# A macaron stack on one core: pieces of the routing placed elsewhere in the mixing tail, marks by units, an own order for the first beats of the last stage

## The chip, the cores and the metric

The kernel runs on one core of one Trainium2 chip. The metric is the time of one execution on the device in microseconds (us); the number compared is the median of several runs. TensorE is called PE, VectorE DVE, ScalarE ACT, GpSimd POOL and SyncE SP, as in the profile.

## The reference, cut to what matters

The input is 4 x 1024 tokens of 128 features. Six layers follow each other, each with a layer norm in front and a residual sum behind:

```python
x = x + 0.5 * moe(ln(x))        # run 0: shared MLP + the two best of 8 experts (128 -> 512 -> 128)
x = x + mix(ln(x))              # 8 heads: h = tanh(a) * h + b along the sequence, then an FFN with gelu
x = x + 0.5 * moe(ln(x))        # run 1: the same MoE weights again
x = x + 0.5 * ternary_ffn(ln(x))    # L1, first half
x = x + linear_attention(ln(x))     # L1: Z = cumsum(v k^T), y = q Z, 16 heads of 8
x = x + 0.5 * ternary_ffn(ln(x))    # L1, second half
```

The MoE's gate is `topk_p, topk_i = top_k(softmax(xf @ Wr), 2)`, so the logits of a token decide which experts' lists it stands in.

## The kernel before, in words

The residual X stays in SBUF. Its 32 blocks of 128 tokens are worked on as TILES = 8 tiles of four blocks (512 columns). Every engine runs a program of its own; the order in each is written out by hand, and engines wait for each other by semaphores. The queues are in order, so a wait holds up all that stands behind it on its engine.

**A MoE run** begins with the routing. For each tile: `find_stats` (L353, DVE), `find_rstd` (L363, POOL: one addition of EPS and one power of -1/2, over the tile's four columns), `normalize_for_route` (L369, DVE, four instructions), `turn_for_route` (L375, PE transposes, from line L193), `copy_for_route` (L381, ACT), `find_logits` (L385, PE, four products of 8 columns, L389). When all eight tiles have logits, `route` (L660, DVE) picks two experts for each token, `find_places` (L394, PE) counts, and `find_spots` (L678, DVE) gives each (token, expert) pair its spot in the lists. Then the lists are inverted: for each of UNITS = 16 units of four columns of spots, `mark` (L707, DVE) writes four pairs of one-hot matrices in f16, `marks_lo` (128 wide, from the spot's low part) and `marks_hi` (92 wide, from its high part, times the token's number), and `add_marks` (L400, PE, L403) adds up their products in one bank. `keep_rows` (L716, DVE) turns the sum into row numbers, with which POOL gathers the lists by indirect DMA (L586).

The marks are spread over the steps of the shared MLP (a step is one `up` and one `down` of a 128-wide chunk, L424 and L437): `units_at` (L318) places units from step 6 in run 0 and from step 8 in run 1, three units for two steps, and `rows_at` places `keep_rows` ten steps behind the first unit's last neighbour. In run 0, DVE and ACT also split the raw expert weights into high and low parts at the even steps (`split_weights`, L499 on ACT, L768 on DVE). After the shared steps of six tiles come 23 lists of 512 rows, then two more shared tiles.

**The mixing** (`mix_pe`, `mix_act`, `mix_pool`, `mix_dve`) runs over 78 slots: 64 slots (HEADS), one for each head of each tile, and 14 more in which tile 7's remaining work runs out: `z_root` (L1292, POOL), `normalize_z` (L1223, ACT), `u_of` (L1416, DVE), `turn_u`, `up`, `down` (L1111, L1117, PE) with `gelu` (L1238, ACT), `h_of` (L1404, DVE), `y_of` (PE), `add_to_x` (L1425, DVE). In these last slots the routing of run 1 is already interleaved for tiles 0 to 6. The placing before is a staircase, one tile a slot:

```python
STATS_AHEAD, NORM_AHEAD, TURN_AHEAD, LOGITS_AHEAD = (HEADS + k for k in (2, 3, 4, 5))
```

Tile i has its stats and its root in slot 66 + i, its normalization in 67 + i, its transpose in 68 + i and its logits in 69 + i. Tile 7's routing waits for the last `add_to_x`, which ends the mixing (`phase_done`); PE does two `up` steps of run 1 ahead of it.

**L1** is one loop over beats (`l1_pe` L1547, `l1_act` L1695, `l1_pool` L1767, `l1_dve` L1835). Tile i does each piece of work at beat lag + 4 i:

```python
ADD_ROWS, STATS_1, TURN_1, UP_1, DOWN_1, BACK_1, TURN_LA, VK, QS, CHUNK_0 = range(10)
```

ADD_ROWS adds the experts' rows of the MoE (`moe_combine`, L652 on DVE, after POOL has fetched them by indirect DMA, L642); STATS_1 to BACK_1 are the first ternary FFN (its `ff_add` is L1847); TURN_LA takes the tile to the attention; VK and QS are its four projections (L1594, L1596, L1608); from CHUNK_0 on, one chunk of 128 tokens a beat is summed: `products` (L1797, POOL), `sums` (L1617, PE), `read_out` (L1863, L1866, DVE). `root` (L1779 to L1784, POOL) stands in front of each normalization (L1691, ACT). In a beat, POOL issues two fetches (from beat 2 on) ahead of the roots of that beat.

## Time and profile before

| | |
|---|---|
| median of 3 runs | 1185.23 us (1183.57 to 1189.68) |
| the profiled execution: its time, its span | 1186.23 us, 1184.5 us |
| busy: PE, DVE, ACT, POOL | 1066.8, 840.4, 669.8, 683.2 us |
| mean granted clock of PE | 0.954 of full speed |
| marks of run 0, run 1 | about 46 to 86 us, 661 to 690 us |
| mixing | about 270 to 642 us, its tail from 600 us |
| L1 | from about 866 us to the end |

The profiled execution takes 1.73 us more than its span, and 1.0 us more than the median. A busy share is an average over stages; which engine's wait ends last is read stage by stage. A granted clock of 0.50 is 1.2 GHz, 1.00 is 2.4 GHz. DMA-issuing instructions on POOL (L586, L642) appear with the time that POOL spends on them.

### The profile page before, as it was taken

The numbers are of one execution on the slowest core, as the hardware profiler recorded it, in microseconds if no ns is written. First come the engines' busy times: TensorE is split into PE (matmuls) and PEld (weight loads), VectorE is DVE, ScalarE is ACT, GpSimd is POOL, SyncE is SP. The second block draws the span as 40 slices with busy tenths as digits, with TensorE's granted clock in tenths as the row PEclk, the third lists the DMA queues.
The fourth block names the chain that finished last, engine by engine and source line by source line (L and its number), as shares of the span: only waits on it lengthen the run. The fifth ranks groups of instructions, "written<-read, shape, count | busy, mean of one in ns | idle before, by whom it ended". The sixth has DMA issues, their size and how long they took to land.

```text
span 1184.5 us, 16414 instructions
## 1 busy us (share of the span) xinstructions
PE 1066.8 (90%) x4800; PEld 731.3 (62%) x4800; DVE 840.4 (71%) x2362; ACT 669.8 (57%) x1265; POOL 683.2 (58%) x786
## 2 busy tenths in 40 slices
PE   6779999998989999999979979999967678999996
PEld 6336778875657677667745448888734445555553
DVE  6785787767867887787765967777762676767661
ACT  2336767765566676667543338777744445545533
POOL 4006556637998888877662046666465665754330
PEclk9989999999999999999987989999996888989998
DMA  8666667741000000000001036877510000000000
GB/s 270 240 261 210 213 214 246 239 127 29 14 14 13 14 14 12 15 5 1 1 19 54 1 117 213 252 241 241 162 53 19 16 16 25 25 12 10 10 18 18
DMA packets 67976, 108.81 MB, mean 92 GB/s; under 512 B 8336, under 2 KB 46224, under 8 KB 67856
## 3 DMA queue, kind: packets, MB, share of 16 engines
q1 hardware_dynamic: 57904, 87.30, 22.1%
q0 software_dynamic: 9984, 20.47, 6.8%
q8 instruction: 39, 0.64, 0.2%
q14 instruction: 49, 0.40, 0.1%
HBM read 81.00 MB, written 28.57 MB: 93 GB/s over the span
## 4 chain that ended last, share of the span: by engine, by line
PE 58%; POOL 17%; DVE 11%; issue 6%; ACT 5%; DMA 2%; POOLq 0%; SPq 0%; DVEq 0%; ACTq 0%
PE bank L193 7%; PE bank L426 3%; PE bank L427 3%; PE bank L428 3%; PE bank L443 3%; PE bank L445 3%; PE bank L444 3%; POOL wr L642 3%; PE bank L1071 3%; PE bank L1077 3%; PE bank L1596 3%; PE bank L424 2%; PE bank L1111 2%; PE bank L1617 2%; POOL got L642 2%
## 5 line engine op out<-in xcount | busy, mean ns | idle before, releaser
L586 POOL DMA_INDIRECT spare_all<-xs,list_row x184 | 191.7, 1042 | 210.9 <-DVE list_row L724 107.4
L781 DVE TENSOR_TENSOR hid_lo<-hid,hid_hi 128x512 fp32r<-128x512 f32 x184 | 127.0, 692 | 75.0 <-ACT hid L528 73.4
L528 ACT ACTIVATE hid<-bank,b_up_of 128x512 f32<-128x512 f32 x184 | 125.6, 684 | 6.5 <-PE bank L428 1.2
L527 ACT ACTIVATE hid_hi<-bank,b_up_of 128x512 fp32r<-128x512 f32 x138 | 95.3, 690 | 47.7 <-PE bank L428 35.2
L642 POOL DMA_INDIRECT got<-ys,y_slots x80 | 87.3, 1091 | 51.0 <-issue 40.7
L193 PEld LDWEIGHTS bank<-ident,spare_all 128*128 128x128 f32 x504 | 64.8, 150 | 78.0 <-issue 57.6
L193 PE MATMUL bank<-ident,spare_all 128*128 128x128 f32 x504 | 82.1, 289 | 26.1 <-DVE spare_all L372 18.0
L1190 ACT ACTIVATE gate_b<-bank,head_rstd 128x128 f32<-128x128 f32 x256 | 73.0, 370 | 55.7 <-POOL head_rstd L1297 55.2
L528 ACT ACTIVATE hid<-bank,cols_sb 128x512 f32<-128x512 f32 x64 | 43.9, 687 | 88.4 <-PE bank L424 79.4
L426 PE MATMUL bank<-xh,wr 128*128 128x512 f32 x184 | 82.4, 448 | 3.5 <-DVE xl L774 3.5
L1863 DVE TENSOR_TENSOR gate_b<-bank,spare_all 128x512 f32<-128x512 f32 x64 | 43.1, 687 | 50.2 <-PE bank L1617 48.0
L443 PE MATMUL bank<-hid_hi,wr 128*128 128x512 f32 x184 | 76.0, 413 | 0.0
L1297 POOL TENSOR_TENSOR head_rstd<-head_var,neg_half 128x4 f32<-128x4 f32 x64 | 72.4, 1131 | 5.3
L424 PE MATMUL bank<-xT,w_shared 128*128 128x512 f32 x128 | 73.1, 661 | 0.8 <-DVEq L1473 0.8
L427 PE MATMUL bank<-xh,wr 128*128 128x512 f32 x184 | 73.0, 397 | 0.0
L428 PE MATMUL bank<-xl,wr 128*128 128x512 f32 x184 | 72.8, 396 | 0.0
L445 PE MATMUL bank<-hid_lo,wr 128*128 128x512 f32 x184 | 72.6, 394 | 0.0
L444 PE MATMUL bank<-hid_hi,wr 128*128 128x512 f32 x184 | 72.5, 394 | 0.0
L1071 PE MATMUL bank<-spare_all,cw_sb 128*128 128x512 f32 x128 | 66.9, 604 | 3.3 <-DVE spare_all L1398 3.2
L1077 PE MATMUL bank<-wz,spare_all 128*128 128x128 f32 x512 | 68.3, 276 | 1.6 <-ACT gate_b L1190 1.6
L437 PE MATMUL bank<-hid,w_shared 128*128 128x512 f32 x128 | 66.7, 611 | 0.0
L1042 PE MATMUL bank<-xh,hid_hi 128*128 128x512 f32 x136 | 65.6, 483 | 1.1 <-DVE xl L1352 0.9
(291 smaller groups left out, 2749.0 us busy)
## 6 DMA issues: line engine op xcount, KB each, us to landing
wr<-wq SPq DMA_DIRECT2D x92, 512.0 KB, 4.7
ys<-spare_all SPq DMA_DIRECT2D x46, 256.0 KB, 5.3
wq<-wr SPq DMA_DIRECT2D x16, 512.0 KB, 5.7
got<-in_w_mlp SPq DMA_DIRECT2D x8, 512.0 KB, 5.9
xs<-spare_all SPq DMA_DIRECT2D x16, 256.0 KB, 2.3
spare_all<-xs,list_row POOLq DMA_INDIRECT x184, 3.7
out_x<-X SPq DMA_DIRECT2D x8, 256.0 KB, 2.3
ys<-in_x SPq DMA_DIRECT2D x1, 1792.0 KB, 10.5
```

Of the source, the lines that this page charges most:

```text
L193: ins = nc.tensor.transpose(out[:, b * P:(b + 1) * P], src(b), ident[:])
L426: nc.tensor.matmul(out[:], w_up(j, 0, c), xh[:, j % 2], start=True, stop=False)
L427: nc.tensor.matmul(out[:], w_up(j, 1, c), xh[:, j % 2], start=False, stop=False)
L428: nc.tensor.matmul(out[:], w_up(j, 0, c), xl[:, j % 2], start=False, stop=True).then_inc(s["up_done"], 1)
L443: nc.tensor.matmul(out[:], w_dn(j, 0, c), hid_hi[:, q], start=(c == 0), stop=False)
L444: nc.tensor.matmul(out[:], w_dn(j, 1, c), hid_hi[:, q], start=False, stop=False)
L445: nc.tensor.matmul(out[:], w_dn(j, 0, c), hid_lo[:, q], start=False, stop=(c == HC - 1)).then_inc(s["down_done"], 1)
L528: nc.scalar.activation(hid[:, n % HC], bank[up_bank(n)][:], ACT.Gelu_apprx_tanh, bias=bias).then_inc(s["gelu_done"], 1)
L586: g.indirect_dma_start(out=xin[:, j % XIN, b], out_offset=None, in_=xs, in_offset=bass.IndirectOffsetOnAxis(ap=list_row[:, n:n + 1], axis=0))\
L642: nc.gpsimd.indirect_dma_start(out=rows_of(i, ring)[:, k, b], out_offset=None, in_=ys, in_offset=bass.IndirectOffsetOnAxis(ap=y_slots[:, k ...
L781: v.tensor_tensor(hid_lo[:, q], hid[:, n % HC], hid_hi[:, q].bitcast(F32), ALU.subtract).then_inc(s["lo_done"], 1)
L1077: ins = nc.tensor.matmul(blk(bank[3 + q % 2], b), blk(o_sb[:, q % 2], b), wz[:, q % NH], start=True, stop=True)
```

## The change: what it does, and the diff

- **Tail.** The staircase is replaced by tables. Stats of tiles 0 to 5 stand in slots 64 to 66, two a slot; one `find_rstd` over 24 columns serves these six tiles in slot 66; tiles 0 to 2 and 3 to 5 are normalized together in slots 67 and 69; only tiles 0 to 3 are turned in the tail (slots 69 and 72), with logits in slots 70, 71, 75 and 76, now ahead of the turns in a slot. Tiles 4 to 6 are turned, and get their logits, at the head of run 1, ahead of tile 7; the four first `up` steps come behind tile 7's logits.
- **Marks.** `marks_hi` is laid out with the unit's four columns innermost, so that one `tensor_tensor` makes it for a whole unit (368 elements in f16, one operand broadcast); the token's number moves to `marks_lo`. PE reads `marks_hi` with a step of four elements. `find_spots` gets one small copy (`spot_hi16`), the constants one more.
- **L1.** In beats 0 to 8 (`fills`) PE and ACT go in an own order: the attention's turn and projections come ahead of the FFN's work of the next tile, and the sums of chunk 0 stand in beat 8 between Q and QT. POOL issues no fetch in beats 2 to 4; the eight of tile 2 come in beat 5 behind that beat's roots, none in beats 6 and 7, two in beat 8, four each in beats 9 and 10, two from then on. Tile 1's rows are added in beat 5, behind tile 0's stats, in place of beat 4.

```diff
-        def find_rstd(pool, steps, s, i):
-            tile = slice(i * TB, (i + 1) * TB)
-            pool.wait_ge(*s.at("stats_ready", i + 1))
...
+        def find_rstd(pool, steps, s, i, tiles=1):
+            those = slice(i * TB, (i + tiles) * TB)
+            pool.wait_ge(*s.at("stats_ready", i + tiles))
+            steps.link(nc.gpsimd.tensor_scalar(ve_all[:, those], mv_all[:, those, 1], EPS, None, ALU.add))
+            nc.gpsimd.tensor_tensor(rstd_all[:, those], ve_all[:, those], neg_half[:, 0:tiles * TB], ALU.pow).then_inc(s["rstd_ready"], tiles)
...
-                for n in range(2):
-                    step(n)
-                turn_for_route(pe, s, TILES - 1)
+                for i in range(TURNED_AHEAD, TILES):
+                    turn_for_route(pe, s, i)
+                    if i > TURNED_AHEAD:
+                        find_logits(pe, s, i - 1)
                 find_logits(pe, s, TILES - 1)
-                for n in range(2, HC):
+                for n in range(HC):
                     step(n)
                 find_places()
...
-                for m in range(TB):
-                    at = u * TB + m
-                    v.tensor_scalar(marks_lo[:, u % 2, m], column_no16[:], spot_lo[:, at:at + 1], None, ALU.is_equal)
-                    ins = v.tensor_scalar(marks_hi[:, u % 2, m], column_no16[:, 0:COLUMNS], spot_hi[:, at:at + 1],
-                                          token_no[:, at % BLOCKS:at % BLOCKS + 1], ALU.is_equal, ALU.mult)
+                at = u * TB
+                by_block = spot_hi16[:, at:at + TB].unsqueeze(1).broadcast_to([P, COLUMNS, TB])
+                v.tensor_tensor(marks_hi[:, u % 2], column_by_block[:], by_block, ALU.is_equal)
+                for n in range(at, at + TB):
+                    ins = v.tensor_scalar(marks_lo[:, u % 2, n - at], column_no16[:], spot_lo[:, n:n + 1],
+                                          token_no[:, n % BLOCKS:n % BLOCKS + 1], ALU.is_equal, ALU.mult)
...
-        STATS_AHEAD, NORM_AHEAD, TURN_AHEAD, LOGITS_AHEAD = (HEADS + k for k in (2, 3, 4, 5))
+        TURNED_AHEAD, NORMED_AHEAD, ROOTS_AHEAD = 4, TILES - 1, TILES - 2
+        STATS_AHEAD = {HEADS: (0, 1), HEADS + 1: (2, 3), HEADS + 2: (4, 5), HEADS + 6: (6,)}
+        NORMS_AHEAD = {HEADS + 3: (0, 1, 2), HEADS + 5: (3, 4, 5), HEADS + 7: (6,)}
+        TURNS_AHEAD = {HEADS + 5: (0, 1), HEADS + 8: (2, 3)}
+        LOGITS_AHEAD = {HEADS + 6: (0,), HEADS + 7: (1,), HEADS + 11: (2,), HEADS + 12: (3,)}
...
+                if n == HEADS + 2:
+                    find_rstd(pool, steps, after, 0, ROOTS_AHEAD)
+                if n == HEADS + 6:
+                    find_rstd(pool, steps, after, ROOTS_AHEAD)
...
+        def parts_at(beat):
+            if beat < CHUNK_0 - 4:
+                return []
+            if beat == CHUNK_0 - 4:
+                return range(TOP * TB, 2 * TOP * TB)
+            first = {CHUNK_0 - 3: 0, CHUNK_0 - 2: 0, CHUNK_0 - 1: 2, CHUNK_0: 4, CHUNK_0 + 1: 4}
...
+                if fills(beat):
+                    if here(TURN_LA) is not None:
+                        l1_take(pe, s, here(TURN_LA), 1, bank[4])
+                    if here(VK) is not None:
+                        project(here(VK), V)
+                        project(here(VK), K)
+                    if here(BACK_1) is not None:
+                        ff_back(here(BACK_1), 0)
+                    if here(QS) is not None:
+                        project(here(QS), Q)
+                        sums(0)
+                        project(here(QS), QT)
+                    if here(UP_1) is not None:
+                        ff_up(here(UP_1), 0)
+                    if here(DOWN_1) is not None:
+                        ff_down(here(DOWN_1), 0)
+                    if here(TURN_1) not in (None, 0):
+                        ff_turn(here(TURN_1), 0)
+                    continue
-                if g is not None:
+                if g is not None and g > 0:
                     sums(g)
...
                     l1_stats(dve, steps, s, here(BACK_1), 1)
+                    if fills(beat):
+                        moe_combine(dve, steps, moe, 1, FETCHED_WIDE)
...
-                if here(ADD_ROWS) not in (None, 0):
+                if here(ADD_ROWS) not in (None, 0, 1):
```

## Rows read from the trace of the kernel before

**Rows 1.** The page's chain that ended last, shares of the span by engine.

```profile
PE 58%; POOL 17%; DVE 11%; issue 6%; ACT 5%; DMA 2%; POOLq 0%; SPq 0%; DVEq 0%; ACTq 0%
```

**Rows 2.** The same chain in order of time, run 0: start, us, what.

```profile
45.12 1.23 DVE wr L768
...
52.39 1.23 DVE wr L768
```

**Rows 3.** Groups by line, DVE, 28 to 110 us: count, busy us, mean ns, idle before.

```profile
L712 DVE TENSOR_SCALAR marks_hi<-column_no,spot_hi,token_no 128x92 f16<-128x92 f16 x64 | 19.5, 304 | 0.0
L711 DVE TENSOR_SCALAR marks_lo<-column_no,spot_lo 128x128 f16<-128x128 f16 x64 | 16.0, 250 | 0.0
...
L697 DVE TENSOR_TENSOR gate_b<-pick,place 128x512 f32<-128x512 f32 x1 | 0.7, 693 | 0.0
...
L728 DVE TENSOR_TENSOR past<-block_no,ends 128x184 f32<-128x184 f32 x1 | 0.3, 344 | 0.0
```

**Rows 4.** Busy time by window, marks of run 1: length, PE, PEld, DVE, ACT, POOL, PEclk, DMA.

```profile
664.00:689.50 25.50, 23.86 (x120) 11.92 (x119) 23.20 (x117) 9.08 (x14) 0.00 (x0) 1.00 0.00 1
```

**Rows 5.** Timeline of the mixing tail and run 1's first work: start, us, engine, line.

```profile
603.95 0.89 DVE L1367 BATCH_NORM_STATS2 o_stats<-bank 128x6 f32<-128x128 f32 x4 [1.45 <-PE bank L193]
...
607.98 0.23 POOL L1296 TENSOR_SCALAR head_var<-o_mv 128x4 f32<-128x4 f32 x1
...
611.93 0.87 DVE L1409 BATCH_NORM_STATS2 z_stats<-pick 128x6 f32<-128x128 f32 x4 [2.90 <-POOL pick L1306]
612.18 1.04 POOL L367 TENSOR_TENSOR rstd_all<-ve_all,neg_half 128x4 f32<-128x4 f32 x1
...
619.90 0.68 DVE L1419 TENSOR_TENSOR t_sb<-t_sb,rows_sb 128x512 f32<-128x512 f32 x1
...
621.36 1.12 PE L193 MATMUL bank<-ident,t_sb 128*128 128x128 f32 x4 [0.47 <-DVE t_sb L1420]
...
624.86 3.60 PE L1111 MATMUL bank<-acc,f_sb 128*128 128x512 f32 x4
...
638.01 1.90 PE L389 MATMUL bank<-cols_sb,xT 128*128 128x8 f32 x16
...
641.46 0.69 DVE L1425 TENSOR_TENSOR X<-bank,X 128x512 f32<-128x512 f32 x1 [3.06 <-PE bank L1049]
...
648.80 0.42 DVE L667 TENSOR_REDUCE top<-bank 128x32 f32<-128x256 f32 x1 [2.48 <-PE bank L389]
```

**Rows 6.** Groups by form, POOL, whole span: count, busy us, mean ns, idle before.

```profile
L1306 POOL TENSOR_TENSOR pick<-pick,gate_b 128x512 f32<-128x512 f32 x32 | 50.3, 1572 | 19.7 <-ACT gate_b L1190 18.9
...
L1783 POOL TENSOR_TENSOR l_shift<-l_mv,l_rstd 128x4 f32<-128x4 f32 x24 | 4.8, 201 | 1.9
L367 POOL TENSOR_TENSOR rstd_all<-ve_all,neg_half 128x4 f32<-128x4 f32 x16 | 16.6, 1037 | 1.3
```

**Rows 7.** PE: timeline of run 0's routing, then two windows (PEclk is 0.50).

```profile
15.50 1.71 PE L389 MATMUL bank<-cols_sb,xT 128*128 128x8 f32 x8
17.07 1.09 PE L193 MATMUL bank<-ident,spare_all 128*128 128x128 f32 x4
...
642.00:644.00 2.00, 1.74 (x2) 0.84 (x3) 1.41 (x9) 0.00 (x0) 0.19 (x1) 0.50 0.00 0
...
904.00:906.00 2.00, 2.00 (x8) 1.34 (x7) 1.97 (x7) 0.59 (x1) 0.00 (x0) 0.50 0.00 0
```

**Rows 8.** Timeline of L1's first beats.

```profile
883.05 0.69 DVE L1847 SCALAR_TENSOR_TENSOR X<-bank,X 128x512 f32<-128x512 f32 x1 [0.15 <-DVE X L652]
...
884.10 0.94 POOL L642 DMA_INDIRECT wr<-ys,y_slots  x1 [0.30 <-issue]
...
888.86 0.23 POOL L1779 TENSOR_SCALAR l_ve<-l_mv 128x4 f32<-128x4 f32 x1
...
890.91 0.23 POOL L1779 TENSOR_SCALAR l_ve<-l_mv 128x4 f32<-128x4 f32 x1
...
908.56 2.09 POOL L1797 TENSOR_TENSOR wa_sb<-spare_all 128x512 f32<-128x512 f32 x2 [10.71 <-ACT spare_all L1725]
```

More of the change, by code:

```diff
@@ L540, in step @@
                     nc.scalar.activation(half_tanh[:], lead[:], ACT.Tanh, scale=0.5).then_inc(s["tanh_ready"], 1)
-            for i in range(TILES if first else 0):
+            for i in range(0 if first else TURNED_AHEAD, TILES):
                 copy_for_route(act, s, i)
-                if i in (4, 6):
+                if first and i in (4, 6):
                     split_weights(i // 2 - 2)
             for n in range(STEPS + TAIL):
-                if not first and n == 2:
-                    copy_for_route(act, s, TILES - 1)
                 if n == STEPS + HC:
@@ L1264, in mix_act @@
                     gelu(two_before, 1)
-                if tile_ahead(n, TURN_AHEAD) is not None:
-                    copy_for_route(act, after, tile_ahead(n, TURN_AHEAD))
+                for i in TURNS_AHEAD.get(n, ()):
+                    copy_for_route(act, after, i)
         def mix_pool(pool, steps, s, moe, after):
@@ L1464, in mix_dve @@
                     u_of(before_it)
-                if tile_ahead(n, NORM_AHEAD) is not None:
-                    if n == NORM_AHEAD:
-                        dve.wait_ge(s["p_in"], HEADS)
-                    normalize_for_route(dve, after, tile_ahead(n, NORM_AHEAD))
-                if tile_ahead(n, STATS_AHEAD) is not None:
-                    find_stats(dve, steps, after, tile_ahead(n, STATS_AHEAD))
+                if n == max(NORMS_AHEAD):
+                    dve.wait_ge(s["p_in"], HEADS)
+                for i in NORMS_AHEAD.get(n, ()):
+                    normalize_for_route(dve, after, i)
+                for i in STATS_AHEAD.get(n, ()):
+                    find_stats(dve, steps, after, i)
             dve.wait_ge(s["tile_done"], TILES)
@@ L1498, in chunk_at, with fills @@
             return g if 0 <= g < CHUNKS else None
+        def fills(beat):
+            return beat < CHUNK_0
+        def parts_at(beat):
[4 more added lines that the diff above has]
+            first = {CHUNK_0 - 3: 0, CHUNK_0 - 2: 0, CHUNK_0 - 1: 2, CHUNK_0: 4, CHUNK_0 + 1: 4}
+            at = 2 * TOP * TB + sum(n for b, n in first.items() if b < beat) + 2 * max(0, beat - CHUNK_0 - 2)
+            return [n for n in range(at, at + first.get(beat, 2)) if n < TOP * TB * (TILES - 1)]
         kv = [w[:].rearrange("p (h a) e -> p h (a e)", h=2) for w in (wa, wb)]
@@ L1805, in l1_pool @@
                     products(chunk_at(beat + 1))
-                ahead, part_no = divmod(2 * beat + TOP * TB // 2, TOP * TB)
-                if beat > STATS_1 and ahead + 1 < TILES:
-                    for n in (part_no, part_no + 1):
-                        moe_fetch(pool, moe, ahead + 1, n, FETCHED_WIDE)
+                if not fills(beat):
+                    for n in parts_at(beat):
+                        moe_fetch(pool, moe, 1 + n // (TOP * TB), n % (TOP * TB), FETCHED_WIDE)
                 if here(BACK_1) is not None:
```

52 lines of the change are left out of this document (36 added, 16 removed).

## The prediction, made before the change was run

> **What bounds the kernel now.** I read the page's chain first: PE carries over half of it, POOL and DVE the next shares [rows 1]. So the time is a relay, and each of the three edits must be priced in its own stage. The chain in order of time shows run 0's marking: two splits of weights on DVE start 7.27 us apart, and between them lie the sixteen mark instructions of two units [rows 2]. In run 1 the window of the marks shows PE busy 23.86 of 25.50 us and DVE 23.20: PE loses 1.64 us to waits, and no more can be won there [rows 4]. The timeline of the tail shows a relay for tile 7, from its stats at 611.93 to the sum at 641.46 to 642.15, and then 6.65 us until the routing starts at 648.80 [rows 5]. In L1's first beats, the root of tile 0 starts at 888.86 although the FFN's sum ended at 883.74: POOL was still issuing fetches [rows 8].
>
> **Marks.** A unit is now four pairs of instructions. Their mean durations are 0.304 and 0.250 us [rows 3]; on the timeline consecutive ones overlap by about 0.09, so they start 0.21 and 0.16 apart, and four pairs take 1.50 us. After the change four `marks_lo` have two operations: they cost like today's `marks_hi`, 4 x 0.22 = 0.88. The new `tensor_tensor` has 368 elements of f16. No row shows a two-source f16 instruction. By 32-bit elements it lies between the 184 and the 512 columns of [rows 3]: 0.344 + 184 x (0.693 - 0.344) / 328 = 0.54 us, 0.45 without the overlap. By bytes, 368 f16 elements are the 184-column f32 row: 0.34, or 0.25. I take the bytes, because today's `marks_lo`, wider than `marks_hi`, is not longer, so columns of f16 can't cost a full step each. A unit then takes 1.13 us instead of 1.50 (0.37 less; 0.17 by elements).
> The Trainium skill (VectorE: DVE Perf Modes, the rule on which mode an instruction takes) lets `tensor_tensor` handle two elements a cycle if all tensors are 16-bit with step one, and never more. By it the unit is the 1.13 above; no run here shows it yet.
> Run 0: five splits are followed by two units each on the chain (from 45.12 on, period 7.27), 10 x 0.37 = **3.7 us**; by elements 1.7. The units at odd steps hide behind the split on ACT. The splits' loads and stores on SP's queue are asked for two periods ahead, which covers a period shorter by 0.7. Run 1: three units take 3.4 us of DVE for two steps of PE, which take 4.4; so DVE stops being the bound and PE regains nearly all of its 1.64: **1.5 us**, with either price. The copy in `find_spots` (0.2) is hidden: in run 0 by the split that follows, in run 1 by PE's steps. The constant is made before the routing, in DVE's wait for logits. `keep_rows`, POOL's gather and the first list follow the marks in both runs, so both gains pass on.
>
> **Tail, DVE and POOL.** Stats of tiles 0 and 1 (1.25 us each) now stand ahead of the last head's stats. These started at 603.95 and ended 2.7 us before POOL took them at 607.98 [rows 5]; they end 1 us later, so nothing moves. Stats 2 to 5 (5.0 us) end at 611.1, and z's stats still start when POOL's last addition is done, 611.93. Then POOL runs the root over 24 columns ahead of z's root. Its price is the unknown. The power over 4 columns takes 1.04 us, a multiplication over 4 takes 0.20 [rows 6]. If width is free: 1.04. If the extra 0.84 grows with the columns: 0.2 + 6 x 0.84 = 5.2 us. An addition over 512 columns takes only 1.57, so the engine has a cheap loop, but the power's loop is not shown. I take 2.0 us, nearer the row of the same operation, and keep both ends. z's root then starts 0.9 later than before.
> **Tail, u to X.** Before, u's first product waited at 619.90 behind other tiles' normalizations, though its input was ready near 617.9; PE then had turns and logits of tiles 1 to 6 between the pieces of the FFN, which began at 624.86 after the turn at 621.36, at a slow clock (3.60 us for four half-matmuls) [rows 5]. After, u's product follows at 617.4 + 0.9; the turn of u ends 1.6 earlier than before; 1.6 us of logits and turns leave the gap in front of `up`, 1.1 the gap in front of its second half, 1.2 that between the `down`s, and the 1.9 us of L389 at 638.01 no longer stand between `h_of` and `y_of` (1.4 of them were on the path). Less one turn or logits that remains in each of two gaps, the last sum comes 5.6 us earlier.
> **Tail, what is late next.** Behind the sum, PE still has logits 2 and 3, then turns 4 to 6 and logits 4 and 5 before tile 7's turn. At full clock (0.43 and 0.87 a tile) this ends just when tile 7 is normalized, 4.2 us after the sum. But in run 0 the same stretch of turns and logits alone runs at 2.45 us a tile, half speed, from end to end [rows 7]; and before the change the clock was down at 642, after some 4 us of small products [rows 7]. The work left over (four turns at 0.89, four logits at 1.57) then takes 9.8 us from about 1.2 after the sum: the routing starts 11.0 behind the sum instead of 6.65, and the four `up` steps, two of them slow, end about when `route` does. That costs 4.4 to 5.7; I take 5.0. Tail: 5.6 - 5.0 = **0.6 us** gained (free width and free clock: 6.5 to 7; 5.2 us for the root: -2.5).
>
> **L1.** After: POOL is free when tile 0's stats are done, so that root starts near 884.9 instead of 888.86, and the first turn of the attention goes into PE's empty time. Tile 1's rows (2.3 us of DVE) now lie between the two stats, so tile 1's root starts at 888.5 instead of 890.91: 2.4 us earlier [rows 8]. From there PE is busy without a break and at a clock of 0.50 [rows 7], and its work up to tile 1's FFN sum is the same but for the turn done earlier (0.9): **3.3 us**. The eight fetches moved behind the roots take 8 x 1.24 = 9.9 us [rows 8], to 900.6; `products` queue behind them and start at 900.7 instead of 908.56, before PE wants the sums. Tile 2's rows land some 4 us after and are added before DVE's first `read_out`. Beats 9 and 10 have two fetches more each (2.5 us), while POOL waits for DVE's stats in the one and has over 5 us before PE needs chunk 3 in the other; if that cover is gone they cost up to 5. Bounds of the term: 0 (PE's slow stretch swallows it) and 7.9 (the first chunk decides).
>
> **Sum.** 3.7 + 1.5 + 0.6 + 3.3 = 9.1 us, from 1186.23 to 1177.1 for an execution like the profiled one; the median of before is 1.0 lower, so 1176.1, rounded to **1176.0**.
>
> **Rivals.**
> - **The power grows with its columns.** For it: 0.84 us more than a multiplication on the same 4 columns. Against: nothing but the cheap addition. z's root is 4 us late instead of 0.9: the tail loses 2.5 instead of gaining 0.6, 1179.2. Chance 0.25.
> - **The clock holds in the tail's end, or L1's beats go by the first chunk.** For it: PE's clock came back in 646 to 648 before. Against: run 0's routing. 4 to 5 us more: 1171.5. Chance 0.18.
> - **The gains don't pass on:** PE's slow clock eats L1's term and marks cost by elements: 9.1 - 3.3 - 2.0 = 3.8, 1181.3. Chance 0.14.
> - **PE pays for the step of four in `marks_hi`, and the kernel gets slower.** Its 128 matmuls read 92 columns at a pitch of about 0.04 us. Read at a quarter of the rate, each costs 0.115 more; 40 of run 0's and all 64 of run 1's are on the path: 12 us. 1176.1 + 12 = 1188.1. It decides from 0.09 us more each. For it: no row shows a moving operand with a step. Against: the reads of f16 are a quarter of the bytes of f32 ones per column pair. Chance 0.03.
> The forecast itself has 0.40.
> The Trainium skill (TensorE: Matmul & The Clock Gate, Part 1) says that the array is at half rate by default and that sustained activity releases it. The trace agrees where PE was empty (0.50 after 884), but run 0's routing stays slow while PE is called busy all the time, which by the page's words would have been released; by that rule the tail would gain 5 us more, the second rival.
>
> **Chances and range.** A measurement of this kernel tells about 0.5% from no change, 5.9 us, so faster means under 1179.3. The forecast, the second rival and half of the first lie there, with a little of the third: 0.40 + 0.18 + 0.12, less a tail, is 0.68. Within 0.5%: the other half of the first, the third, most of the fourth: 0.30. Slower: 0.02. The range goes from 1169.5 (second rival with L1's upper bound in part) to 1183 (third rival with the root's price in part).
>
> **What would show it.** Marks: the distance of two splits in run 0 is 6.5 us instead of 7.27, the new `tensor_tensor` lasts 0.34 (0.54 would be by elements), L403 stays at 0.20, PE in run 1's marks is busy over 98%. Tail: the power over 24 columns lasts 2 us; L1425's last record comes 5.6 us earlier against the last head; the routing starts 11 us behind it, with a clock of 0.50. L1: the distance from tile 0's FFN sum to tile 1's falls from 34.6 to 31.3 us. The forecast is wrong if the root takes over 4 us, if the routing starts within 8 us of the sum, or if L1's distance doesn't fall.

## The result, and the profile after

The changed kernel took 1178.39 us (median of 12 runs, 1173.78 to 1183.12); the kernel before took 1187.45 us beside it (1183.57 to 1192.89). The ratio is 0.9912, with a 95% interval of 0.9894 to 0.9930: faster, by 8.3 to 12.6 us. The forecast was 1176.0, within 1169.5 to 1183.0. The sum came out nearly right. Of its terms only one did: one was nothing where 1.5 us were forecast, one was twice its size, and one was 3 to 4 instead of 0.6, by two errors of opposite sign. Medians and ratios, here and below, leave out two runs, one of the kernel before (1207.96 us) and one of m2_tail_only in the next section (1198.13), that were slower than the rest at a lower clock.

The profiled execution of after took 1181.54 us, only 4.7 less than the one of before. So one execution can't be read for the whole gain; the stages below are compared over several kernels that share a part. The page of after, its instructions and its chain by engine:

```profile
span 1179.8 us, 16312 instructions
PE 1069.1 (91%) x4800; PEld 736.5 (62%) x4800; DVE 836.2 (71%) x2269; ACT 668.7 (57%) x1265; POOL 678.7 (58%) x776
PE 60%; POOL 16%; DVE 9%; issue 9%; ACT 5%; DMA 0%; POOLq 0%; SPq 0%; DVEq 0%; ACTq 0%
```

Against [rows 1], DVE lost 2 points of the chain and PE gained 2; which stages they come from, the views below say.

**Marks, run 0.** Pieces of the chain in order of time (start, us, what), then DVE's groups from 28 to 104 us (busy us, mean ns, idle us before), both of after:

```profile
45.48 1.23 DVE wr L773
46.97 0.89 DVE marks_lo L717 x4
48.12 0.91 DVE marks_lo L717 x4
52.15 1.23 DVE wr L773
```

```profile
L717 DVE TENSOR_SCALAR marks_lo<-column_no,spot_lo,token_no 128x128 f16<-128x128 f16 x64 | 15.6, 307 | 0.0
L715 DVE TENSOR_TENSOR marks_hi<-column_by_block,spot_hi 128x368 f16<-128x368 f16 x16 | 5.5, 342 | 0.0
```

Two splits start 6.67 us apart (7.27 in [rows 2]). Four `marks_lo` take 0.89 to 0.91 us, and a unit starts 1.15 us behind the one before. The new instruction takes 0.342 us on 368 f16 columns: the same as the f32 row of 184 columns in [rows 3].

**Marks, run 1.** The windows with the marks, of after, with the columns of [rows 4], and the groups of L407, the matmuls that read the marks (min/median/max ns, first and last start):

```profile
655.00:690.00 35.00, 35.00 (x143) 18.54 (x143) 27.47 (x103) 13.30 (x20) 0.00 (x0) 1.00 0.00 0
664.00:689.50 25.50, 25.50 (x121) 14.30 (x120) 18.85 (x73) 9.13 (x14) 0.00 (x0) 1.00 0.00 1
L407 PE MATMUL bank<-marks_hi,marks_lo x128: 242/263/267, 47.9 to 689.3; 128*128 128x92 f16 x128
```

The same line in the kernel before was L403:

```profile
L403 PE MATMUL bank<-marks_hi,marks_lo x128: 202/204/287, 47.9 to 689.2; 128*128 128x92 f16 x128
```

PE has no idle time left, as forecast, but the stage is no shorter (41.8 us before and 42.1 after, column E of the table below). Each matmul has become 0.059 us longer in its own record, and 0.039 us longer in the mean distance from the start of one to the start of the next (0.082 instead of 0.043). Run 1 has 64 of them: 2.5 us more work of PE, in place of 1.64 us of waits.

**Tail.** The timeline of after, with the columns of [rows 5]:

```profile
610.54 0.87 DVE L1419 BATCH_NORM_STATS2 z_stats<-pick 128x6 f32<-128x128 f32 x4
610.91 4.20 POOL L371 TENSOR_TENSOR rstd_all<-ve_all,neg_half 128x24 f32<-128x24 f32 x1
615.08 0.23 POOL L1281 TENSOR_SCALAR z_var<-z_mv 128x4 f32<-128x4 f32 x1
618.90 0.69 DVE L1429 TENSOR_TENSOR t_sb<-t_sb,rows_sb 128x512 f32<-128x512 f32 x1
622.85 3.76 PE L1119 MATMUL bank<-acc,f_sb 128*128 128x512 f32 x4
638.63 0.69 DVE L1435 TENSOR_TENSOR X<-bank,X 128x512 f32<-128x512 f32 x1 [1.68 <-PE bank L1057]
645.07 3.42 PE L393 MATMUL bank<-cols_sb,xT 128*128 128x8 f32 x16
648.53 0.42 DVE L670 TENSOR_REDUCE top<-bank 128x32 f32<-128x256 f32 x1 [5.05 <-PE bank L393]
```

The power over 24 columns takes 4.20 us and holds z's root from 611.9, when z's stats are done, to 615.08. The sum of X (start 638.63) is nevertheless 28.1 us behind z's stats, where it was 29.5 [rows 5]; the routing is 9.9 us behind the sum, where it was 7.3 from start to start.

**L1.** The timeline of after, with the columns of [rows 8]:

```profile
885.91 0.69 DVE L1912 SCALAR_TENSOR_TENSOR X<-bank,X 128x512 f32<-128x512 f32 x1 [3.38 <-PE bank L193]
888.01 0.23 POOL L1842 TENSOR_SCALAR l_ve<-l_mv 128x4 f32<-128x4 f32 x1 [10.67 <-DVE l_mv L1893]
891.63 0.23 POOL L1842 TENSOR_SCALAR l_ve<-l_mv 128x4 f32<-128x4 f32 x1 [1.39 <-DVE l_mv L1893]
903.99 2.10 POOL L1860 TENSOR_TENSOR wa_sb<-spare_all 128x512 f32<-128x512 f32 x2
909.11 3.02 PE L1642 MATMUL bank<-wa_sb,wz 128*128 128x512 f32 x4
916.40 0.69 DVE L1912 SCALAR_TENSOR_TENSOR X<-bank,X 128x512 f32<-128x512 f32 x1 [0.35 <-issue]
```

Tile 0's root starts 2.10 us behind the FFN's sum (5.81 in [rows 8]), and tile 1's FFN sum follows at 30.5 us instead of 34.6. POOL's wait of 10.67 us in front of the root shows that POOL is no longer what holds it.

**Stages.** Distances in the profiled execution of each kernel, us, each between two starts: from run 0's routing (its first reduction of logits) to the cast of `list_row` (A), from the routing to DVE's first copy of a list's result out of PSUM (B), from z's stats to the last sum of X (C), from there to run 1's routing (D), from there to run 1's cast of `list_row` (E), from tile 0's FFN sum to tile 1's (F), from there to the last sum (G). The kernels are those of the next section.

| kernel | A | B | C | D | E | F | G |
|---|---|---|---|---|---|---|---|
| before | 54.4 | 88.4 | 29.5 | 7.3 | 41.8 | 34.6 | 263.1 |
| after | 49.9 | 87.5 | 28.1 | 9.9 | 42.1 | 30.5 | 260.0 |
| m0_whole (after, again) | 49.9 | 83.3 | 25.3 | 7.5 | 41.9 | 30.5 | 260.6 |
| m1_marks_only | 50.0 | 85.3 | 29.5 | 7.3 | 41.6 | 34.8 | 263.4 |
| m2_tail_only | 54.3 | 89.9 | 25.5 | 7.3 | 42.2 | 28.9 | 262.6 |
| m3_l1_only | 53.5 | 88.9 | 32.3 | 8.6 | 41.8 | 30.4 | 260.2 |
| m4_no_tail | 51.5 | 87.2 | 32.4 | 7.4 | 41.6 | 30.5 | 261.4 |
| m12_fetch_only | 54.4 | 88.4 | 29.5 | 7.4 | 41.8 | 31.0 | 263.3 |
| m5_pairs | 51.7 | 85.4 | 28.3 | 7.4 | 39.7 | 30.4 | 261.4 |
| m6_late_loads | 49.9 | 83.5 | 28.4 | 7.3 | 42.0 | 30.5 | 261.4 |
| m7_roots | 50.9 | 84.8 | 24.4 | 7.4 | 42.0 | 30.3 | 260.4 |
| m8_turns | 51.3 | 84.8 | 26.1 | 9.3 | 42.2 | 30.3 | 259.9 |
| m9_all | 51.3 | 88.0 | 23.1 | 9.3 | 40.0 | 30.5 | 261.4 |
| m10_no_turns | 51.1 | 87.4 | 22.2 | 7.4 | 39.7 | 30.4 | 260.6 |

A, E, F and G agree within 1.8 us between kernels that have the same part, but for F in m2_tail_only. B, C and D don't: kernels with the same code there differ by up to 4.2 us. One pair of executions can't price a term that lies in them.

Much of this spread goes with PE's granted clock. In every kernel it falls to 0.50 near z's stats and comes back to 1.00 while PE works on tile 7; it falls again near the last sum. The times below (us) are read from the traces, with m0 to m12 for the kernels' full names: when it came back, counted from z's stats, and when it fell, counted from the start of the last sum.

| tail | kernels | clock back at | C |
|---|---|---|---|
| old | before, m1, m12 | 16.1 to 16.4 | 29.5 |
| old | m3, m4 | 22.2, 22.5 | 32.3, 32.4 |
| new | m0, m2 | 15.2, 15.8 | 25.3, 25.5 |
| new | after, m5, m6 | 21.0 to 21.9 | 28.1 to 28.4 |
| new, two more turns ahead | m8 | 15.4 | 26.1 |
| root in pieces | m7 | 17.8 | 24.4 |
| root in pieces, two more turns ahead | m9 | 12.5 | 23.1 |
| root in pieces | m10 | 12.3 | 22.2 |

| kernels | clock down at | D |
|---|---|---|
| before, m1, m4, m12 (old tail) | 0.3 to 0.5, back at 3.7 to 3.9 | 7.3 to 7.4 |
| m3 (old tail) | 0.1, back at 13.8 | 8.6 |
| m0, m2, m5, m6, m7, m10 | 7.0 to 7.3 | 7.3 to 7.5 |
| after, m8, m9 | 3.0 to 3.1 | 9.9, 9.3, 9.3 |

With the clock back at a like time, the new tail's C is about 4 us shorter than the old one's, early or late.

### The profile page after: what moved, and what is told of

It reads as the page before. It is cut to its first block, busy times and chain, and to the rows that moved or that the text cites. A ratio compares the mean times of both kernels' runs of the same rounds, so it can differ in the third digit from the quotient of the medians.

```text
span 1179.8 us, 16312 instructions
## 1 busy us (share of the span) xinstructions
PE 1069.1 (91%) x4800; PEld 736.5 (62%) x4800; DVE 836.2 (71%) x2269; ACT 668.7 (57%) x1265; POOL 678.7 (58%) x776
## 4 chain that ended last, share of the span: by engine, by line
PE 60%; POOL 16%; DVE 9%; issue 9%; ACT 5%; DMA 0%; POOLq 0%; SPq 0%; DVEq 0%; ACTq 0%
PE bank L193 7%; PE bank L430 4%; PE bank L428 4%; PE bank L432 4%; PE bank L431 3%; PE bank L447 3%; PE bank L449 3%; PE bank L448 3%; POOL wr L645 3%; PE bank L441 3%; PE bank L1085 3%; PE bank L1079 3%; PE bank L1119 2%; PE bank L1125 2%; PE bank L1642 2%
## 5 line engine op out<-in xcount | busy, mean ns | idle before, releaser
L589 POOL DMA_INDIRECT spare_all<-xs,list_row x184 | 194.5, 1057 | 212.0 <-DVE list_row L729 105.8
L645 POOL DMA_INDIRECT got<-ys,y_slots x80 | 87.3, 1092 | 51.1 <-issue 41.1
L193 PE MATMUL bank<-ident,spare_all 128*128 128x128 f32 x504 | 82.1, 290 | 22.2 <-DVE spare_all L376 14.4
L430 PE MATMUL bank<-xh,wr 128*128 128x512 f32 x184 | 83.3, 453 | 6.6 <-issue 4.7
L428 PE MATMUL bank<-xT,w_shared 128*128 128x512 f32 x128 | 69.2, 630 | 0.0
```

The lines of the kernel that those rows point to most:

```text
L193: ins = nc.tensor.transpose(out[:, b * P:(b + 1) * P], src(b), ident[:])
L428: nc.tensor.matmul(out[:], w_shared[:, 0, c * P:(c + 1) * P], xT_all[:, tile_of(k)], start=True, stop=True).then_inc(s["up_done"], 1)
L430: nc.tensor.matmul(out[:], w_up(j, 0, c), xh[:, j % 2], start=True, stop=False)
L589: g.indirect_dma_start(out=xin[:, j % XIN, b], out_offset=None, in_=xs, in_offset=bass.IndirectOffsetOnAxis(ap=list_row[:, n:n + 1], axis=0))\
L645: nc.gpsimd.indirect_dma_start(out=rows_of(i, ring)[:, k, b], out_offset=None, in_=ys, in_offset=bass.IndirectOffsetOnAxis(ap=y_slots[:, k ...
```

## The experiments

The kernels ran in three groups, each on one chip together with the kernel before: m1 to m4 (12 runs each); m5 to m8 (6 each); and m0 (5), m9 (4), m10 (6) and m12 (12). Medians of before in the three groups: 1189.17, 1187.12 and 1188.42 us. The ratios are to before, with their 95% intervals; they are the measured ones and not quotients of the medians, from which they differ by up to 0.002 (2.3 us). Microseconds gained are given by the ratio.

### Each part alone

The marks alone: of the change, only the hunks of `marks_hi`, `column_by_block`, `spot_hi16` and `mark`.

```
-        marks_hi = sb("marks_hi", [P, 2, TB, COLUMNS], F16)
+        marks_hi = sb("marks_hi", [P, 2, COLUMNS, TB], F16)
...
+                v.tensor_tensor(marks_hi[:, u % 2], column_by_block[:], by_block, ALU.is_equal)
```

> The kernel before with the marks' part alone. My prediction's theory: 3.7 us from run 0 and 1.5 from run 1, so 5.2 us faster than before. The rival, read from the changed kernel's trace: in run 0 the row numbers come 4 us earlier, but the first experts' weights don't, so nothing of it is left by 120 us; in run 1 PE's strided reads (0.26 us instead of 0.20 each) eat the 1.6 us that DVE gives back. So within 1.5 us of before.

Measured: 1187.07 us, ratio 0.9975 [0.9948, 1.0002]. A is 50.0, as in after, and E is 41.6, against 41.8: nothing in run 1, without the rest of the change as well as with it.

The tail alone: `find_rstd` with `tiles`, the tables `STATS_AHEAD` to `LOGITS_AHEAD`, and the loops of PE, ACT, DVE and POOL that read them.

```
+        TURNED_AHEAD, NORMED_AHEAD, ROOTS_AHEAD = 4, TILES - 1, TILES - 2
...
+                if n == HEADS + 2:
+                    find_rstd(pool, steps, after, 0, ROOTS_AHEAD)
```

> The kernel before with the part on the mixing tail and on run 1's head alone. My prediction's theory: 0.6 us faster with a root of 2.0 us; with the 4.20 us that the changed kernel's trace shows for it, about 1 us slower. The rival (the clock and the shorter chain carry more than one profile of each shows): 3 us faster or more.

Measured: 1188.45 us, ratio 0.9977 [0.9943, 1.0012]. C is 4.0 shorter and D the same as before: the clock did not take back what was gained. F is 28.9 without the change of L1, which no step of the prediction expected. The clock can account for it: in this window of L1's first beats it was at 1.00, where before it was at 0.50 [rows 7]. It was back at 1.00 15.4 us behind tile 0's FFN sum, and before 28.4 us behind it; 13.0 us at half speed are worth 6.5 us at most, an estimate, and F is 5.7 shorter.

```profile
900.00:904.00 4.00, 3.75 (x21) 2.66 (x21) 2.85 (x7) 3.09 (x6) 0.00 (x0) 1.00 0.00 0
```

L1 alone, from `fills` and `parts_at` on:

```
+                if fills(beat):
+                    if here(TURN_LA) is not None:
+                        l1_take(pe, s, here(TURN_LA), 1, bank[4])
...
-                if here(ADD_ROWS) not in (None, 0):
+                if here(ADD_ROWS) not in (None, 0, 1):
```

> The kernel before with L1's order of the first beats alone. My prediction's theory: 3.3 us faster, with 31.3 us between the FFN sums of tile 0 and tile 1. The rival, from the whole traces, in which L1 is some 6 us shorter: most of the 9 us of the whole change are here, 6 to 9 us faster.

Measured: 1184.93 us, ratio 0.9984 [0.9949, 1.0019]. F is 4.2 and G 2.9 shorter, yet the ratio gives only 1.9 us, and its interval ends at 6.1. C and D, where this kernel has no edit, are 2.8 and 1.3 longer than before in the profiled execution; how often that happens one profile can't say. Its runs spread from 1179.67 to 1197.10 us, almost twice as far as those of the whole change, so the ratio says little of the size.

Marks and L1 without the tail's part:

```
-        TURNED_AHEAD, NORMED_AHEAD, ROOTS_AHEAD = 4, TILES - 1, TILES - 2
...
+        STATS_AHEAD, NORM_AHEAD, TURN_AHEAD, LOGITS_AHEAD = (HEADS + k for k in (2, 3, 4, 5))
```

> Marks and L1 together, without the part on the tail. If the parts add up and the tail gives nothing or costs 1 us, this is as fast as the whole change or 1 us faster; if the tail carries 3 us or more, it is slower than the whole change by as much. My prediction's theory: 8.5 us faster than before.

Measured: 1181.91 us, ratio 0.9920 [0.9892, 0.9947], 9.5 us. That is more than the two parts alone give together (3.0 + 1.9), and within their intervals, which are 3 to 4 us wide on each side. By the theory written down for this kernel, a tail worth 3 us or more makes it that much slower than the whole change. In two different groups the whole change gave 10.4 and 13.2 us, so the tail would be worth 1 to 4 us, and the runs alone don't say which. Runs of single parts show the sign of a term here, hardly its size.

The whole change a second time, in the third group:

```
(no edit: after.py)
```

> The whole change again, unchanged, so that it stands beside the next three on one chip. Both theories: 0.991 of before, within the interval of the first measurement. The way from the last sum of the mixing to the routing of run 1 is either about 7.3 or about 9.9 us, by whether PE's clock has fallen by then.

Measured: 1175.28 us, ratio 0.9889 [0.9855, 0.9922]. Between its profiled execution (1171.89 us) and that of after lie 9.6 us, with the same instructions: 4.2 in B, 2.8 in C, 2.4 in D. C and D go with the clock, as the tables above show. PE in windows of 1.5 us behind the sum: first three of after, whose sum started at 638.63, then two of this kernel, whose sum started at 631.21:

```profile
640.13:641.63 1.50, 1.21 (x12) 0.97 (x11) 0.66 (x6) 1.07 (x2) 0.56 (x2) 1.00 0.05 16
641.63:643.13 1.50, 1.50 (x11) 1.50 (x10) 0.76 (x3) 0.27 (x1) 0.70 (x1) 0.54 0.00 0
643.13:644.63 1.50, 1.50 (x8) 1.50 (x9) 0.35 (x2) 0.32 (x1) 0.00 (x0) 0.50 0.16 45
```

```profile
634.21:635.71 1.50, 1.50 (x15) 1.44 (x14) 0.76 (x3) 0.59 (x1) 0.70 (x1) 1.00 0.00 0
637.21:638.71 1.50, 1.50 (x13) 1.50 (x13) 0.03 (x1) 1.47 (x2) 0.00 (x0) 0.84 0.49 135
```

In after the clock was down 3 us behind the sum; here it fell 7 us behind it, when most logits were done. The last 16 logit products (L393) take 3.42 us in after and 2.03 here:

```profile
636.61 2.03 PE L393 MATMUL bank<-cols_sb,xT 128*128 128x8 f32 x16
```

### What run 1's marks cost PE

`marks_hi` in pairs: DVE still writes two columns of spots side by side, so its instruction keeps steps of one element, and PE reads with a step of two instead of four.

```
-        marks_hi = sb("marks_hi", [P, 2, COLUMNS, TB], F16)
+        marks_hi = sb("marks_hi", [P, 2, 2, COLUMNS, 2], F16)
...
-  marks_lo[:, u % 2, m], marks_hi[:, u % 2, :, m],
+  marks_lo[:, u % 2, m], marks_hi[:, u % 2, m // 2, :, m % 2],
```

> The whole change with marks_hi laid out in pairs of columns, so that PE reads it with a step of two elements in place of four, from one tensor_tensor as before. Theory (the step of four makes PE's reads cost 0.082 us of pitch in place of 0.043): the 128 products go back to about 0.20 us each, and in run 1 the way from the routing to the row numbers falls from about 41.6 to 39.2 us. Rival (PE was not what set this stage any more): the distance stays within 0.5 us.

Measured: 1171.48 us, ratio 0.9864 [0.9834, 0.9894]. Its matmuls, and DVE's instruction:

```profile
L407 PE MATMUL bank<-marks_hi,marks_lo x128: 202/203/283, 48.3 to 682.6; 128*128 128x92 f16 x128
L716 DVE TENSOR_TENSOR marks_hi<-column_by_block,spot_hi 128x368 f16<-128x368 f16 x16 | 5.5, 343 | 0.0
```

The matmul is back at 0.203 us and at 0.042 from one to the next, DVE's price stays, and E is 39.7 instead of 42.1: the 2.4 us that the pitch says. The step of four is the cause, and a step of two costs nothing. Against before (41.8), E is now 2.1 us shorter: with PE's price gone the term of run 1 is there, where 1.5 had been forecast.

### What holds the first list in run 0

In after's profile 4.5 us were won up to `list_row` but only 0.9 up to the first list's result. One theory was that loads for later stages, which SP issues ahead of run 0's first list, make its weights late. They were moved behind the first lists:

```
+                if first and 4 <= j < 4 + len(late_loads):
+                    dst, name = late_loads[j - 4]
+                    sp.dma_start(dst[:], t[name]).then_inc(c_dma, 16)
...
-            for dst, name in late_loads:
-                sp.dma_start(dst[:], t[name]).then_inc(c_dma, 16)
```

> The whole change with the five late weight loads and the filling of ys moved behind the loads of the first lists' weights on SP's queue. Theory (in run 0 the marks' gain is lost to the first lists' weights, which queue behind 3.8 MB of other loads): PE's wait of 2.8 us at the second list goes, and the first stored list comes 2 us or more earlier against the routing (85 us after it or less; 87.5 in the changed kernel, 88.4 before). Rival (POOL's gathers set it): no change of that distance.

Measured: 1176.41 us, ratio 0.9903 [0.9875, 0.9931]: as after. The first weights are issued 4.5 us earlier (after, then this kernel), and B is 83.5:

```profile
89.17 0.28 SPq L891 DMA_DIRECT2D wr<-wq  x1
```

```profile
84.71 0.37 SPq L891 DMA_DIRECT2D wr<-wq  x1
```

But m0_whole has 83.3 with the loads where they were, and m9_all and m10_no_turns have 88.0 and 87.4 with the loads moved. PE's gap there differs in size and in what ended it. After, m0_whole, m9_all (in brackets: idle us, releaser):

```profile
102.75 0.80 PE L430 MATMUL bank<-xh,wr 128*128 128x512 f32 x1 [2.80 <-issue]
```

```profile
97.01 0.66 PE L193 MATMUL bank<-ident,spare_all 128*128 128x128 f32 x4 [0.47 <-DMA spare_all<-xs,list_row]
```

```profile
95.25 0.65 PE L193 MATMUL bank<-ident,spare_all 128*128 128x128 f32 x4 [2.06 <-DMA spare_all<-xs,list_row]
```

So the theory isn't borne out. Here too the clock goes with the spread. In A it did not fall between 6 and 50 us behind the routing in after, m0, m1 and m6, whose A is 49.9 to 50.0; in m4, m8 and m10 it fell twice, and A is 51.1 to 51.5; before, m2 and m12, with the old marks, have two such falls as well, and A is 54.3 to 54.4. With one fall A is 50.9 (m7) and, with the old marks, 53.5 (m3). So with a like clock the marks give 2.6 to 3.4 us up to `list_row`, as five periods shorter by 0.60 do (3.0), and the rest of after's 4.5 goes with the clock. In B the clock fell 65 to 71 us behind the routing in after, m4, m9 and m10 (87.2 to 88.0), in each next to a wait of PE of 1.8 to 2.8 us, and not there in the six others with the new marks (83.3 to 85.4). What makes PE wait in those four stays open.

### What the wide root costs the tail

The root over six tiles cut into pieces, each as soon as its tiles' stats are there, and z's root no longer behind all of them:

```
+        ROOTS_AT = {HEADS: (0, 1), HEADS + 1: (1, 1), HEADS + 2: (2, 1), HEADS + 3: (3, 3), HEADS + 6: (6, 1)}
...
-                if n == HEADS + 2:
-                    find_rstd(pool, steps, after, 0, ROOTS_AHEAD)
-                if n == HEADS + 6:
-                    find_rstd(pool, steps, after, ROOTS_AHEAD)
+                if n in ROOTS_AT:
+                    find_rstd(pool, steps, after, *ROOTS_AT[n])
```

> The whole change with the one root for six tiles taken apart: tiles 0, 1 and 2 one by one in POOL's gaps in slots 64 to 66, tiles 3 to 5 together behind z's root. Theory (the power takes about 0.16 us a column and stands on tile 7's path): z's root starts near z's stats' end (within 0.5 us in place of 3.2 us), and the last sum of the mixing comes 3 us earlier against the last head. Rival (the chain from u to the sum is set by PE's slow clock): less than 1 us.

Measured: 1171.41 us, ratio 0.9861 [0.9838, 0.9884]. POOL's timeline of this kernel:

```profile
607.97 1.04 POOL L371 TENSOR_TENSOR rstd_all<-ve_all,neg_half 128x4 f32<-128x4 f32 x1
609.17 0.23 POOL L1282 TENSOR_SCALAR z_var<-z_mv 128x4 f32<-128x4 f32 x1 [0.16 <-DVE z_mv L1423]
611.74 2.40 POOL L371 TENSOR_TENSOR rstd_all<-ve_all,neg_half 128x12 f32<-128x12 f32 x1
```

z's root now waits for nothing but z's stats, and the power over 12 columns, 2.40 us, runs behind it. C is 24.4: below the five kernels with the wide root and this order of turns (25.3 to 28.4, mean 27.1), and 2.7 below their mean, where the wide root had held z's for 3.2. The clock came back here 17.8 us behind z's stats, between the two groups of the wide root; on the line between these groups C would be 26.5, so about 2 us is the root's share, an estimate. The expected 3 us were too many.

### What lies behind the last sum

The prediction said that four turns and logits left behind the sum cost 5 us because of a slow clock. Here two more turns, and two more logits, stand ahead of the sum:

```
-        TURNED_AHEAD, NORMED_AHEAD, ROOTS_AHEAD = 4, TILES - 1, TILES - 2
+        TURNED_AHEAD, NORMED_AHEAD, ROOTS_AHEAD = 6, TILES - 1, TILES - 2
-        TURNS_AHEAD = {HEADS + 5: (0, 1), HEADS + 8: (2, 3)}
+        TURNS_AHEAD = {HEADS + 5: (0, 1), HEADS + 8: (2, 3), HEADS + 10: (4, 5)}
-        LOGITS_AHEAD = {HEADS + 6: (0,), HEADS + 7: (1,), HEADS + 11: (2,), HEADS + 12: (3,)}
+        LOGITS_AHEAD = {HEADS + 6: (0,), HEADS + 7: (1,), HEADS + 11: (2,), HEADS + 12: (3, 4), HEADS + 13: (5,)}
```

> The whole change with tiles 4 and 5 turned in slot 74, where PE waits for h, and their logits in slots 76 and 77; only tiles 6 and 7 are turned at the head of run 1. Theory (what stands behind the last sum costs twice, at a slow clock): the routing starts 8.3 us or less behind the last sum, in place of 9.9, and the last sum moves by less than 0.5 us. Rival: what goes from behind the sum comes back ahead of it, and the way from the last head to the routing stays.

Measured: 1175.47 us, ratio 0.9907 [0.9878, 0.9936]: as after. D is 9.3, longer than the 7.3 to 7.5 of four of the five kernels that leave more behind the sum. The clock fell 3.0 us behind the sum here, and 7.0 to 7.3 in those four. In after it fell at 3.1 as well, and against after D is 0.6 shorter, while C, beside m0 and m2 with a like clock, is 0.6 to 0.8 longer: what went from behind the sum came back ahead of it, as the rival said.

### Together

All four edits of this section at once, then the same without the turns of m8_turns:

```
+ m5_pairs, m6_late_loads, m7_roots, m8_turns
```

> The whole change with marks in pairs, the root taken apart, tiles 4 and 5 turned in slot 74, and the late loads behind the first lists' loads. If the four repairs add up as the distances of their stages do (2.4 us from run 1's marks, 2.4 us or more from run 0's lists, 3.7 us from z's root, 1 us from the turns), it is 9 us faster than the whole change, near 0.983 of before. Rival (what one stage gives is taken back by waits for weights in the lists): as fast as the best single repair, 0.986.

```
+ m5_pairs, m6_late_loads, m7_roots
```

> The last kernel without its part on the turns of tiles 4 and 5. Theory (what stands behind the last sum costs): 1 us slower than with it. Rival (the turns only move their cost ahead of the sum): the same within 0.5 us, or faster.

Measured: 1173.12 us, 0.9856 [0.9816, 0.9896], and 1170.59 us, 0.9838 [0.9802, 0.9874]. The second is the fastest kernel of this study, 4.7 us below the whole change in the same group (1175.28); the intervals overlap, but E (39.7) and C (22.2, the shortest of all) show both edits in their places. The four edits don't add up: 9 us below the whole change were expected, and 2.2 came. D is 9.3 with the turns and 7.4 without, as in m8_turns, and C 23.1 and 22.2. In both kernels with the turns the clock fell 3 us behind the sum, in six of the seven with the new tail and without them 7 us behind it. By that count the turns may well bring the earlier fall, but it is not shown: after has it without them.

### POOL's order in L1 alone

Of L1's part, only where POOL issues its fetches: eight behind the roots of the first beats.

```
-                ahead, part_no = divmod(2 * beat + TOP * TB // 2, TOP * TB)
...
+                if fills(beat):
+                    for n in parts_at(beat):
+                        moe_fetch(pool, moe, 1 + n // (TOP * TB), n % (TOP * TB), FETCHED_WIDE)
```

> The kernel before with POOL's new order of fetches in L1 alone; PE, ACT and DVE keep their old order. Theory (the first root waited for the fetches, and that is the gain): the FFN sums of tiles 0 and 1 stand 31 us apart in place of 34.6. Rival (PE's order is the gain: chunk 0's sums one beat earlier): 34 us or more. From tile 1's sum to the end it stays at 263 us, since chunk 0's sums stay in beat 9; in the whole change that is 260.

Measured: 1185.46 us, ratio 0.9970 [0.9944, 0.9997]. The roots and both FFN sums of this kernel:

```profile
883.38 0.69 DVE L1864 SCALAR_TENSOR_TENSOR X<-bank,X 128x512 f32<-128x512 f32 x1 [0.15 <-PE bank L193]
885.49 0.23 POOL L1794 TENSOR_SCALAR l_ve<-l_mv 128x4 f32<-128x4 f32 x1 [9.67 <-DVE l_mv L1845]
887.54 0.23 POOL L1794 TENSOR_SCALAR l_ve<-l_mv 128x4 f32<-128x4 f32 x1
914.38 0.68 DVE L1864 SCALAR_TENSOR_TENSOR X<-bank,X 128x512 f32<-128x512 f32 x1
```

Tile 0's root starts 2.11 us behind the sum instead of 5.81 [rows 8], and F is 31.0, so 3.6 of the 4.1 us of F come with POOL's new order of fetches alone. The clock may have a share in them: it was back at 1.00 25.0 us behind tile 0's FFN sum here and 28.4 before, and 3.4 us at half speed are worth 1.7 at most, an estimate. With L1's whole part an earlier clock brings nothing more: in m7 and m8 it was back 18.3 us behind that sum, and F is 30.3. So L1's part shortens F beside the kernel before, and not beside m2_tail_only, whose 28.9 come with the old order and an early clock.

G is 263.3, as before: the 2.4 us of G need the new orders on PE, ACT and DVE. Here too the clock goes with it: its next fall in L1 lasts 10.2 us in the four kernels with the old orders and 6.8 in the ten others. Which of the two brings the other is not shown.

## Why the prediction was right, and where it wasn't

**The total** holds: 1176.0 against 1178.39 and 1175.28. The gain forecast was 9.1 us; the medians differ by 9.1, and the ratio gives 10.4. It holds partly by luck: of four terms one was right, and the errors of the others have both signs. By two of the prediction's own three signs the forecast was wrong: the root took over 4 us, and in four of the five kernels with the new tail the routing started within 8 us of the sum.

**Marks, run 0: 3.7 forecast, 3.4 measured** up to the first list's result (mean of B over the seven kernels with the new marks and the loads in the old place, 85.5, against 88.9 over the four with the old marks), and 3.4 up to `list_row` (mean of A, 50.8 over the ten kernels with the new marks against 54.2 over the four with the old). The step from bytes was right: 0.342 us, not 0.54. This is the rule of the Trainium skill (VectorE: DVE Perf Modes, section What auto-detection actually checks) that `tensor_tensor` handles two elements a cycle on 16-bit tensors with step one; the trace now agrees, since 368 f16 columns take 0.342 us and 184 f32 ones 0.344. The unit takes 1.15 us (1.13 forecast). "Both gains pass on" holds for run 0 on average, and not in one execution: after's own lost 3.6 of 4.5 us on the way.

**Marks, run 1: 1.5 forecast, nothing measured.** The step that failed is "PE regains nearly all of its 1.64": it did, in that PE is busy without a break, but the work to be done grew by 64 x 0.039 = 2.5 us. The price of the step of four was put at nothing in the sum. The prediction had this mechanism as its last rival, at 0.115 us each and 12 us in all, and gave it 0.03, to decide from 0.09. It is there at a third of that price. A rival with a threshold should also be entered in the sum as a term with a range: at any value between 0 and 0.09 the rival is "false" and the term is wrong. The forecast "L403 stays at 0.20" was the row that would show it, and it showed it.

**Tail: 0.6 forecast, 3 to 4 measured.** Two steps failed, in opposite directions. First, the root: 4.20 us instead of 2.0. With 1.04 us for 4 columns, 2.40 for 12 and 4.20 for 24, each column costs 0.16 us; "nearer the row of the same operation" was the wrong choice, since the surplus of 0.84 us over a multiplication of the same width was the only row about the operation itself, and it grows with the columns. The gain up to the sum was 3.5 (C: 30.6 on average over the five kernels with the old tail, 27.1 over the five with the new one), or about 4 with a like clock, instead of 5.6, and the first rival was true in its mechanism. With the root in pieces about 2 us more came. Second, what lies behind the sum: 5.0 forecast as lost, against 0.3 (D: 7.6 on average with the old tail, 7.9 with the new). "At half speed from end to end" was read from run 0's routing, where the same instructions run; in the tail they follow big products, and the clock held on for 3 and 7 us in the two executions shown. That was the first half of the second rival. The Trainium skill (TensorE: Matmul & The Clock Gate, Part 1) says that sustained activity releases the clock; by that rule this loss was not to be expected, and in four kernels of five it is absent. After's own profile has half of it: 9.9. And the clock fell all the same in each, 3 to 7 us behind the sum. Had the first rival alone come true, the tail would have lost; with both, the net is 3 to 4, and the tail alone measured 2.7 (0.9977, with no change inside its interval).

**L1: 3.3 forecast, about 6.5 in the stages.** F is the 3.3 and a little more: 34.6 to 30.5, where 31.3 was named; up to 1.7 us of it may be the clock's earlier return (25.3 to 25.6 us behind tile 0's sum in most of these kernels, 28.4 before), which the prediction did not count on. The other 2.4 us (G, 263.1 on average over four kernels with the old order, 260.7 over ten with the new) were in no step. The prediction ended its path at tile 1's FFN sum and priced the rest as "the same but for the turn", though the same edit puts chunk 0's sums into the first beats. That the new orders on PE, ACT and DVE bring it is shown by m12_fetch_only; which of the three was not tried, and the shorter fall of the clock goes with it. The step that POOL's fetches held tile 0's root was right, and is most of F. The steps about DVE's rows between the two stats were not needed for it: without them F is 31.0.

**Sum of stages.** By the averages, 3.4 + 0 + 3.2 + 6.5 = 13.1 us. The two measurements of the whole change give 10.4 and 13.2 (ratios 0.9912 and 0.9889). L1's own run gives less than its stages (1.9, at most 6.1); that difference is not settled. That F can be as short with the old order and an early clock (28.9 in m2_tail_only) may be part of it; one execution doesn't show how often that happens.

**Of the rivals**: the first and the tail's half of the second both happened, and cancelled. The third, that the gains don't pass on, did not, except for run 1's marks. Slower was ruled out.

## What to carry to other kernels

When a faster layout for one engine's write changes another engine's read, price the read in the sum and not as a rival: here it took back all of one term, and a layout in between (pairs) kept both prices. A helper made wider to save instructions should be asked what each column costs and who stands behind it on the queue: the root for six tiles saved POOL 1.3 us of busy time against the four pieces of the kernel m7_roots (three of 1.04 and one of 2.40, against 4.20), and delayed the critical tile by 3.2. And where kernels with the same code differ by 4 us in a stage, a term in that stage is sized over several kernels, and between those in which the clock fell and came back at a like time, not from one pair of profiles.

## What the runs showed of the hardware

- **A matmul's moving operand with a step.** At a granted clock of 1.00, 92 columns of f16 took 0.204 us with step one (before), 0.203 with step two (m5_pairs) and 0.263 with step four; from one to the next 0.043, 0.042 and 0.082. The Trainium skill (SBUF — State Buffer, in its section Door 1: The DMA port swizzle) says that two hits in a line of 16 bytes keep the full rate, and that one may stride up to 8 bf16 elements for free; by it a step of four costs nothing for elements of this width. The trace disagrees, and the measurement decides.
- **POOL's power** takes 1.04, 2.40 and 4.20 us over 4, 12 and 24 columns of f32 on 128 partitions.
- **The clock behind the same work is not the same each time.** The same instructions of the tail's end ran at 1.00 until 3 us behind the sum in one execution and until 7 in the other, and the distance to the routing was 9.9 and 7.5. Where the clock came back some 6 us later behind z's stats, the way to the last sum was 2.6 to 3.1 us longer, with either tail. L1's first beats ran at 0.50 until 911 us in before and at 1.00 from 899 in m2_tail_only, whose L1 is the same code, and F was 5.7 us shorter: more than the 4.1 that L1's own change brought there.
- **A long stage of the same code varies by 2 us.** From run 1's cast of `list_row` to the last copy of a list's result the fourteen profiled executions took 171.3 to 173.5 us; what decides it was not looked into.
